# A five-layer graph network: layer 0's gathers by destination skip the rows of blocks that nobody reads

## The reference, cut to what matters

```python
N, E, K, H, L = (6250, 3125, 31250, 128, 2)
def _conv_layer(x, he_attr, row, col, stoich, W, att, bias):
    xt = x @ W
    et = he_attr @ W
    a = xt[row] @ att[:H] + et[col] @ att[H:]
    a = jax.nn.leaky_relu(a, NEG_SLOPE)
    amax = jax.ops.segment_max(a, col, num_segments=E)
    ex = jnp.exp(a - amax[col])
    den = jax.ops.segment_sum(ex, col, num_segments=E)
    alpha = ex / den[col]
    ...
    m1 = (Binv[col] * stoich * alpha)[:, None] * xt[row]
    eout = jax.ops.segment_sum(m1, col, num_segments=E)
    m2 = (Dinv[row] * stoich * alpha)[:, None] * eout[col]
    nout = jax.ops.segment_sum(m2, row, num_segments=N)
    return nout + bias
```

## Time and profile before

| what | value |
|---|---|
| median of the two runs shown | 11,827.02 us (11,825.48 and 11,828.57) |
| span of the profiled execution, first to last instruction | 11,822.6 us |
| first and last gather of the first pass `a` (start) | 1,016.1 and 2,227.6 us |
| first and last gather of the second pass `a` (start) | 3,604.4 and 4,817.9 us |
| indirect gathers in the launch | 7,424, of which 1,856 in the two passes `a` |

### The profile page before, as it was taken

How to read it: one execution, slowest core, us unless ns; L and a number is a source line. 1 busy time by engine, 2 the same in 40 slices (tenths; PEclk the granted TensorE clock), 3 DMA queues, 4 the chain that set the end, 5 groups by cost and what they waited for, 6 DMA issues and landing times. The chain is left out here.

```text
span 11822.6 us, 182142 instructions
## 1 busy us (share of the span) xinstructions
PE 8182.0 (69%) x47949; PEld 6566.7 (56%) x47949; DVE 8126.2 (69%) x31101; ACT 5076.1 (43%) x14757; POOL 7702.8 (65%) x7673
## 2 busy tenths in 40 slices
PE   7895777666656777555545555788886677767776
PEld 5675777544436777444434554666665444545554
DVE  9765888655556777655562222688887788878888
ACT  4553444322224444222231111466665566646665
POOL 2445777677766777677757777355653677747775
PEclk8876666655556667666567677899998666556566
DMA  1112222355542222578844444344443444434443
GB/s 17 9 20 55 53 53 53 74 130 130 128 110 60 53 53 53 134 203 205 205 131 130 132 131 128 101 145 146 147 146 100 132 134 134 133 105 134 133 134 114
DMA packets 712736, 1297.08 MB, mean 110 GB/s; under 512 B 196563, under 2 KB 369073, under 8 KB 711217
## 3 DMA queue, kind: packets, MB, share of 16 engines
q0 software_dynamic: 282368, 575.57, 22.4%
q1 hardware_dynamic: 388992, 615.05, 16.6%
q10 hardware_dynamic: 40368, 94.82, 2.1%
HBM read 1050.01 MB, written 234.74 MB: 109 GB/s over the span
## 5 line engine op out<-in xcount | busy, mean ns | idle before, releaser
L615 POOL DMA_INDIRECT WK<-tab,IDX x4640 | 4624.3, 997 | 1688.7 <-issue 1345.2
L1454 POOL DMA_INDIRECT B<-tab,IDX x1856 | 1774.7, 956 | 848.5 <-issue 507.3
L615 POOL DMA_INDIRECT H<-tab,IDX x928 | 878.9, 947 | 644.1 <-DVE H L1260 346.4
L1473 DVE TENSOR_REDUCE WK<-PS 128x4 f32<-128x1024 f32 x928 | 1130.4, 1219 | 190.9 <-PE PS L1599 188.6
L1584 ACT ACTIVATE B<-B 128x33 f32<-128x33 f32 x5568 | 1211.2, 308 | 8.0
L839 ACT ACTIVATE WK<-WK 128x128 f32<-128x128 f32 x1856 | 592.6, 390 | 1289.5 <-DMA WK<-tab,IDX 1265.9
L921 PE MATMUL PS<-WK 128*128 128x129 f32 x3712 | 744.2, 362 | 429.6 <-DVE WK L974 208.8
L1632 PEld LDWEIGHTS PS<-B,H 128*128 128x128 f32 x3712 | 819.8, 330 | 283.0 <-issue 274.3
L1632 PE MATMUL PS<-B,H 128*128 128x132 f32 x3712 | 880.7, 430 | 87.3 <-DVE ACC L1486 87.3
L921 PEld LDWEIGHTS PS<-WK 128*128 128x128 f32 x3712 | 638.3, 259 | 527.1 <-DVE WK L974 268.0
L921 PE MATMUL PS<-WK,B 128*128 128x129 f32 x3712 | 829.1, 394 | 12.1 <-ACT WK L1160 8.5
(11 more groups left out here) (426 smaller groups left out, 19037.9 us busy)
## 6 DMA issues: line engine op xcount, KB each, us to landing
H<-onehots SPq DMA_DIRECT2D x232, 768.0 KB
B<-onehots SPq DMA_DIRECT2D x232, 384.0 KB
onehots<-B ACTq DMA_DIRECT2D x232, 384.0 KB
WK<-tab,IDX POOLq DMA_INDIRECT x4640
onehots<-WK SPq DMA_DIRECT2D x232, 256.0 KB
B<-onehots SPq DMA_DIRECT2D x232, 256.0 KB
WK<-onehots SPq DMA_DIRECT2D x232, 256.0 KB
onehots<-B SPq DMA_DIRECT2D x232, 128.0 KB
```

The source lines that it names most:

```text
L615: po.indirect_dma_start(out=G[:, g % n, k, :], out_offset=None, in_=table, in_offset=bass.IndirectOffsetOnAxis(ap=IDX[:, idx, t:t + 1], ax ...
L1454: po.indirect_dma_start(out=eG[:, g % 4, k, :], out_offset=None, in_=tab[TW3], in_offset=bass.IndirectOffsetOnAxis(ap=IDX[:, o, t:t + 1], ...
L1473: ve.tensor_reduce(eM2[:, g, b:b + 2, 2 * i:2 * i + 2, 1] if isinstance(g, int) else eM2[:, bass.ds(g, 1), b:b + 2, 2 * i:2 * i + 2, 1].re ...
```

## The change

A fourth index list is made for pass `a` alone. While the blocks of the pairs are worked out for the order by destination, the PE product that counted blocks for one partition now gives the count on all 128 (`blocks_pe`), and DVE makes from it a row `beyond`: 0 for a pair of a block below 25 (EB), and 49 * 128 = 6,272 for any other. `ordered_ve` stores the larger of this and the old index as `IDX[:, 3, :]`. Pass `a` gathers by that list, and each gather names 6,271 as the largest index allowed, with the rule that a larger one is skipped without an error. Since the slots of skipped rows would keep what lay there, `a_ve` clears the ring before each pass. The number 6,271 is handed to a gather in a register of POOL's: the built program has one register move ahead of each of the 1,856 gathers (1,858 such moves on POOL in place of 2), and everything else on POOL stands as it did.

```diff
--- before.py
+++ after.py
@@ -16,6 +16,7 @@
 K = 106250
 D = 128
 RF = 3125
+EB = 25
 NB = 49
 C0 = 830
 REST = K - 128 * C0
@@ -121,7 +122,7 @@
         LOW = sb("LOW", [128, 2, NT])
         WGT = sb("WGT", [128, 2, NT])
         BLK = sb("BLK", [128, 2, NT // 2], I32)
-        IDX = sb("IDX", [128, 3, NT], I32)
+        IDX = sb("IDX", [128, 4, NT], I32)
         NV = sb("NV", [128, NB, 12])
         WT = sb("WT", [128, 1400])
         WK = sb("WK", [128, 8704])
@@ -224,6 +225,7 @@
         gi, gl, go = (WK[:, 1568 + NT * i:1568 + NT * (i + 1)].bitcast(I32) for i in range(3))
         from_ = WK[0:NB, 4400:4400 + NT // 2]
         spread = B2[:, 12740 - NT:12740].bitcast(I32)
+        beyond = WK[:, 4900:4900 + NT // 2]
         idle = IDX[:, :, :].rearrange("p o t -> p (o t)")[:, 0:30 * 64].bitcast(F32)
         bt = lambda v: v.rearrange("p (t b) -> p b t", t=TC)
         ew = words[:, 1, :]
@@ -473,7 +475,7 @@
             pe.matmul(PS[0:NB, 0, 490 + o:491 + o], UF[0:NB, 0:NB], cbq[0:NB, o:o + 1], start=True, stop=True).then_inc(s_bq, 1)
             pe.wait_ge(s_bc, o + 1)
             pe.wait_ge(s_ev, 2 * NP)
-            pe.matmul(PS[0:1, 4 + o, 0:NT // 2], ONF[0:NB, 0:1], from_, start=True, stop=True).then_inc(s_bl, 1)
+            pe.matmul(PS[:, 4 + o, 0:NT // 2], ONF[0:NB, :], from_, start=True, stop=True).then_inc(s_bl, 1)
 
         def blocks_ve(ve, o):
 
@@ -485,6 +487,8 @@
             own(ve, "ve", ve.tensor_copy(bsq[0:NB, o:o + 1], PS[0:NB, 0, 490 + o:491 + o]))
             ve.tensor_scalar(from_, io464[0:NB, :], bsq[0:NB, o:o + 1], None, ALU.is_ge).then_inc(s_bc, 1)
             ve.wait_ge(s_bl, o + 1)
+            if o == 0:
+                ve.tensor_scalar(beyond, PS[:, 4, 0:NT // 2], float(EB) + 0.5, float(NB * 128), ALU.is_ge, ALU.mult)
             ve.tensor_scalar(BLK[0:1, o, :], PS[0:1, 4 + o, 0:NT // 2], -1.0, None, ALU.add).then_inc(s_blr, 1)
 
         def ordered_pe(pe, o):
@@ -512,6 +516,9 @@
             own(ve, "ve", ve.tensor_scalar(go, gi, 7, None, ALU.arith_shift_right))
             own(ve, "ve", ve.scalar_tensor_tensor(gi, go, 0.0, spread, ALU.is_lt, ALU.mult))
             own(ve, "ve", ve.tensor_tensor(IDX[:, o, :], go, gi, ALU.add))
+            if o == 0:
+                ve.tensor_tensor(IDX[:, 3, :].rearrange("p (j w) -> p j w", w=2), IDX[:, 0, :].rearrange("p (j w) -> p j w", w=2),
+                                 beyond.unsqueeze(2).broadcast_to([128, NT // 2, 2]), ALU.max)
             if o == 1:
                 own(ve, "ve", ve.tensor_scalar(IDX[:, 2, :], IDX[:, 1, :], RF - 1, None, ALU.min))
 
@@ -607,14 +614,15 @@
 
             return base + 64 * (g // n + 1) if isinstance(g, int) else (g - r % n) * (64 // n) + (base + 64)
 
-        def rows_po(po, p, idx, table, G, g):
+        def rows_po(po, p, idx, table, G, g, last=None):
 
             n = RING[ORDER[p]]
+            skip = {} if last is None else dict(bounds_check=last, oob_is_err=False)
             for k in range(4):
                 t = 4 * g + k
                 po.indirect_dma_start(
                     out=G[:, g % n, k, :], out_offset=None, in_=table,
-                    in_offset=bass.IndirectOffsetOnAxis(ap=IDX[:, idx, t:t + 1], axis=0)).then_inc(s_ring[g % n], 16)
+                    in_offset=bass.IndirectOffsetOnAxis(ap=IDX[:, idx, t:t + 1], axis=0), **skip).then_inc(s_ring[g % n], 16)
 
 
 
@@ -723,7 +731,7 @@
             at, ring = raised_before(p)
             for g in range(NG):
                 po.wait_ge(S.r, at.r + g - 7)
-                rows_po(po, p, 0, tab[TW], aG, g)
+                rows_po(po, p, 3, tab[TW], aG, g, NB * 128 - 1)
 
         def a_ve(ve, p, l):
             at, ring = raised_before(p)
@@ -818,6 +826,7 @@
                     ve.tensor_tensor(aDD[:, rm, 4:6], aY[:, qm, :, 0], aY[:, qm, :, 2], ALU.subtract).then_inc(S.m5, 1)
 
             ve.memset(aNB, -BIG)
+            ve.memset(aG.rearrange("p a b c -> p (a b c)"), 0.0)
             own(ve, "ve", ve.tensor_scalar(aVA, LOW[:, 0, :], 0.0, None, ALU.is_ge))
             meet(ve)
             sweep(8, body)
```

## The result

The changed kernel took 11,941.21 us in the median of two runs (11,940.48 and 11,941.94) against 11,827.02 us. The ratio on record is 1.0103, with a 95% interval of 1.0073 to 1.0132; the quotient of the two medians is 1.0097 and lies inside it. The prediction was 11,852 us with a range of 11,650 to 12,300; the kernel is 1% slower, which is within 2%, and 89 us above the forecast. The span of the profiled execution grew by 117.6 us, to 11,940.2.

The account below looks back on a forecast made before the run. POOL's rate of issuing gathers was taken to bound the passes `a`. Register moves of 19 us and other work of 6 made 25 us on the span of 11,822.6; with 4.4 around it 11,852 us, range 11,650 to 12,300.

Parts of the forecast that it names:

- POOL's rate sets the length of a pass `a`: In both passes `a`, POOL issues a gather each 1.307 us, 5.23 us a group; 928 of them fill the 1,212 us.
- The bytes are worth nothing by themselves: In passes `a`, 64.6 MB of skipped reads save no time by themselves, since all 928 gather instructions of a pass stay.
- The register move, 19 us: On POOL ahead of each pass `a` gather: 0.01 us each, 1,856 x 0.01 = 19 us; ends 0 and 130 us.
- The comparison and the skipped rows, taken at the price of a plain gather: On POOL in passes `a`: checking indices and skipping rows add nothing to a plain gather's 946 to 952 ns.
- unchanged within 0.1 us: Forecast case for passes `a`: a gather's cost changes by no more than 0.1 us; chance 0.47.
- The work beside the gathers, 6.4 us: DVE's sort instructions 2.2 us, PE's weights 0.6, ring clearing 0 ahead of the first pass and 3.6 ahead of the second.
- The cheap rival: In passes `a`, skipped rows cost POOL less, DVE then sets 4.5 us a group: 174 us gained, about 11,675; chance 0.17.
- The dear rival: In passes `a`, checked gathers cost POOL more; 0.128 us each makes 2% slower, 0.30 us gives about 12,395; chance 0.32.
- What would show it: Signs: pass `a` gather medians by half, 0.30 us gap, ACT's wait, 65 MB fewer read, L830 to first gather 3.6 us longer.

Follow-up runs that it names:

- kernel without gathers in the tail: Kernel before the change, but POOL issues no gather for the last 119 groups of each pass `a` and ACT doesn't wait for them: 11,610.9 us, 0.9824.
- all live: Changed kernel with EB 49 in place of 25, so no index lies beyond the limit and all rows move: 11,938.2 us, 1.0104 to the kernel before.
- all skipped: Changed kernel with EB 0 in place of 25, so every index of the passes `a` lies beyond the limit: 11,926.9 us, 1.0099 to the kernel before.
- one-register kernel: Changed kernel with the limit put into a POOL register once, without the 1,856 register moves: 11,930.1 us, 1.0103 to the kernel before.
- kernel with the list and without the limit: Changed kernel with EB 49 and no limit on the gathers, fourth list and ring clearing kept: 11,815.6 us, 0.9993 to the kernel before.
- fewer-rows kernels: Pass `a` gathers of 64 rows (limit in second pass), then 32 (limit in first), old list: 11,808.6 and 11,701.8 us beside 11,812.8 and 11,826.9.

## Why the prediction was right, step by step

*POOL's rate sets the length of a pass `a`.* Right. The limit, and the smaller number of rows, changed a gather's time on POOL and the pass with it; the kernel without gathers in the tail runs at DVE's 4.48 and 4.26 us a group, and bytes alone (all live against all skipped) give 11 us, which is within the intervals.

*The bytes are worth nothing by themselves.* Right; with 2 GB/s the second half of a pass did not get shorter.

*The register move, 19 us.* Mis-sized: zero, by the gaps and the one-register kernel. It was 19 of the 25 us that the forecast added, so that the forecast pointed to slower at all was in good part luck. Its low end was taken for possible, and the row that spoke for it, the same gap with a wait and without one, was the better guide than the 0.01 us from DVE's list.

*The comparison and the skipped rows, taken at the price of a plain gather.* This is the term of the sum that was mis-sized. The limit costs 0.052 us a gather, 1,856 x 0.052 = 97 us, and with the 0.064 us by which the first pass's mean rose, as more of its gathers are long, some 11 more: 108 us, as the two passes grew (107.5). The medians lie 114 us apart and the spans 118. It lies within the "unchanged within 0.1 us" of the forecast, which is why the range held. I took the widths of the rows as a sign that gathers don't vary; they say nothing of the number of indices or of what is done to each. The scatter's 1,557 ns, on the other side, was a sign that the form counts.

*The work beside the gathers, 6.4 us.* The instructions took what was said, and the clearing is hidden ahead of the first pass (5.9 us from L828 to the first gather, 5.4 from L820 before) and on the path ahead of the second, with 4.8 us in place of 3.6, as the idle time ahead of it was left out. The sum itself doesn't show in the times of the kernel with the list and without the limit.

*The cheap rival.* Shown not to happen: skipped rows are not spared at all. The fewer-rows kernels show how little there was to spare: of a gather's 947 ns only some 80 hang on the number of rows between 32 and 128. Continued from 64 and 32 to no rows at all, that line comes to some 0.83 us, and the fixed part of the limit's price lifts it to 0.86: an estimate, but over the 0.82 that this rival needed for its full gain (1.13 less the gap of 0.30). The Trainium skill's rule that GpSimd computes a descriptor pair for each operation ("DMA: Bandwidth & Descriptors", section "SWDGE vs HWDGE vs iDMA") doesn't lead to a saving here: a fully skipped gather takes 1,005 ns where a live one takes 1,004, and its packets stay, with 4 B left of each skipped row. What POOL does for such a row was not seen; its time and the packets were.

*The dear rival.* Its mechanism is what happened, at 0.052 us a gather where it needed 0.128 to be slower by 2%. That the price comes with the limit and not with the skipping is shown by the all-live kernel.

*What would show it.* The medians, the halves of a pass and the gap told the story as said; ACT's wait did not shrink. Two signs were ill chosen: the DRAM line of the page was the wrong place to look for the bytes, and the distance from L830 to the first gather could not grow by 3.6 us (it is 1.4 us after 1.0), since the clearing, L829, stands ahead of L830.

## What to carry to other kernels

Where GpSimd's rate of indirect gathers sets the pace, as in the passes `a` here, a gather has to be left out whole: skipped rows leave all of its cost and fewer rows leave nearly all of it (857 of 940 ns with a quarter of them), and a limit on the indices adds 5%. Ahead of such a change ask what the gather's time hangs on, bytes, rows or the instruction, and measure the one that the trace doesn't vary. Of work whose result nobody reads, the whole of the loop's turns is worth far more (10%) than the loads alone (1.8%).

## What the runs showed of the hardware that I had not expected

Gathers that fetch one and the same row 128 times kept the DMA engines busy for 0.90 of the time at 42 GB/s, against 0.24 at 53 GB/s for scattered rows, and cost the launch 3.2%. An indirect gather on GpSimd has a large fixed part: 857 ns at the shortest with 32 rows and 940 with 128, both in the second pass. And a gather whose rows are all skipped still sends its packets: 16 of 32 B in place of 16 of 4,224 B, which is 4 B a row.
